# Windowed transformer on Trainium2: row-shift copies in eight pieces, two attention tiles without unused fronts, feed-forward rows normalised by ScalarE

## Chip, cores and metric

One core of one Trainium2 chip. The metric is the device time of one execution in microseconds (us). Three runs of the kernel before are shown, and one execution of it was profiled.

## What is computed

The program has four stages on x of shape (2, 2048, 128). The last one, with more than seven tenths of the time, is the only one that the change touches: a transformer of six layers over a window of 32 positions, with 16 heads of 64. Its reference, cut to what matters:

```python
def shift_tokens(t):
    a, s = jnp.split(t, 2, -1)
    s = jnp.pad(s, ((0, 0), (1, 0), (0, 0)))[:, :-1]
    return jnp.concatenate([a, s], -1)

def attn_layer(x, Wqkv, qs, ksc, Wo):
    q, k, v = jnp.split(x @ Wqkv, 3, -1)          # then 16 heads of 64
    q, k = l2norm(q) * qs, l2norm(k) * ksc
    q = q * cos * scale + rotate_half(q) * sin * scale
    k = k * cos / scale + rotate_half(k) * sin / scale
    return local_attention(q, k, v) @ Wo          # own window of 32 and the one before

def ffn_layer(x, g, bln, W1, b1, W2, b2):
    xn = (x - mean(x)) / jnp.sqrt(var(x) + 1e-05) * g + bln
    a, gate = jnp.split(xn @ W1 + b1, 2, -1)      # 341 units each
    return a * jax.nn.gelu(gate, approximate=False) @ W2 + b2

for i in range(DEPTH):                            # DEPTH = 6
    x = attn_layer(shift_tokens(x), ...) + x
    x = ffn_layer(shift_tokens(x), ...) + x
```

## The kernel before

All of it is in `windowed_transformer` (L1170), written in Bass with one program for each engine and semaphores between them; the order of each engine's work is written out by hand. A tile is 128 positions (J = 16 of them) of one batch row (B = 2): U = 32 tiles a layer, called units here, numbered u = 2 j + b. The residual lies in SBUF in two parts: its left 64 columns in `xs`, its right 64 in `xb`. The token shift of the right half is a copy by DMA: `xb` shifted down by one partition into columns 64 to 127 of `xs`, by `shift` (L1403, 127 partitions) and `shift_rows` (L1407, the row that crosses to the next tile), both on SyncE's queue. At the stage's start all 16 positions' tiles go in one pair; in a layer one pair follows each two units of attention, and one pair each of the eight groups of the feed-forward. SyncE also copies `early_values` (L1411): the values of the window before a tile, that the attention of half the windows reads.

A layer starts with a **prologue** (L1524 on GpSimd, L1672 to 1684 on TensorE). GpSimd copies a tile of `xs` to `x_tile`, TensorE transposes it and projects it with Wqkv in six chunks of 512 columns, three matmuls each for precision. ScalarE squares the q and k chunks, VectorE turns them (L1965: times the rotary tables) and sums the squares. GpSimd adds the two rotary terms (`rotate`, L1464), makes the inverse norm of k (`floor_k`, `newton_k`) and scales (`scale_k`, `scale_q`). Then comes the **loop over the 32 units**, in which each engine works two tiles ahead: while unit u is attended, the k and q of u+1 are transposed, and u+2 is transposed, projected, squared and turned. The part that serves later tiles is called a tile's front. Before, it runs in every unit, for tiles 32 and 33 too, whose results are not used. A unit ends with `residual` (L2005).

The **feed-forward** takes eight groups of G4 = 4 units. For each group VectorE makes statistics (`group_stats`), variance, an inverse root in ten Newton steps (`group_rstd`, L64 to 82, started from an integer), and normalises the rows (`group_normalise`, L2090). TensorE transposes them (L1726); ScalarE applies the layernorm's scale and bias and rounds (`split_group`, L1918, L1920) and VectorE makes the low part (L2095). `hidden_units` (L1742) has three chunks of hidden units, gate columns in bank S and value columns in bank PT, three matmuls each. ScalarE applies Gelu (L1937), VectorE multiplies (`gate`, L2101), `outputs` (L1769) multiplies by W2, and VectorE adds to the residual (`add_outputs`, L2146), two groups later. Meanwhile GpSimd prepares the next layer's attention (`prepare_attention`, L1313: weights split in two at L1329 and L1331, tables scaled at L1336).

What sets the order at the seams: the feed-forward's first statistics stand behind the last unit's residual on VectorE, and the first x tile of the next layer waits for the last piece of the shift:

```python
pool.wait_ge(shift_main, DMA * (l * SHIFTS + 1))      # with one increment at the start
pool.wait_ge(shift_row, DMA * (l * SHIFTS + 1))       # and SHIFTS = J + GROUPS a layer
nc.gpsimd.tensor_copy(xcur[:], xs[:, 0, 0, :])        # L1524
```

## Time and profile before

| | us |
|---|---|
| median of 3 runs | 5956.59 (5954.01 to 5966.02) |
| the profiled execution | 5959.97 |
| its span, first to last instruction | 5958.0 |
| mean granted TensorE clock (1 is full speed) | 0.909 |
| busy: TensorE matmul, VectorE, ScalarE, GpSimd | 5089.0, 4327.4, 3775.4, 2536.1 |
| windowed stage, its six layers' first transposes | 1626.7, 2344.9, 3059.6, 3775.0, 4490.0, 5205.9 |

The rows of the trace use these names: PE is TensorE, PEld its weight load, DVE VectorE, ACT ScalarE, POOL GpSimd, SP SyncE, and SPq SyncE's DMA queue. Buffers of this stage begin with d_. "out<-in" are an instruction's operands, x and a number its count, and a bracket at the end says how long the engine stood idle before it and what released it. Times are microseconds from the span's start, a mean of one is in ns. Layer 0 is the first of the six, and its unit 31 ends with the residual at about 2229.

### The profile page before, as it was taken

Reading aid. Unit: us, or ns where it says so; the run is one execution under the profiler, and the core shown is the slowest. Engines: PE = TensorE matmul, PEld = TensorE weight load, DVE = VectorE, ACT = ScalarE, POOL = GpSimd, SP = SyncE. Lnnn points to the kernel's source line nnn. Section 1 sums busy time; section 2 is a strip of 40 time slices with the busy share of each in tenths; the row PEclk is TensorE's granted clock in tenths of the full one; section 3 lists DMA queues with packets and bytes.
Section 4 is the critical chain, followed back from the end, with each engine's and each line's share of the span. In section 5 each row is a group of like instructions: output and inputs, shape, how many; then the busy total and the mean of one; then the engine's idle time right before and its main releaser. Section 6 shows DMA issues by size and latency. Waiting matters only on the chain. (4 is left out here: it accounts for less than half of the span.)

```text
span 5958.0 us, 148484 instructions
## 1 busy us (share of the span) xinstructions
PE 5089.0 (85%) x41656; PEld 4226.5 (71%) x41656; DVE 4327.4 (73%) x11808; ACT 3775.4 (63%) x12267; POOL 2536.1 (43%) x3943
## 2 busy tenths in 40 slices
PE   5987868997089996999869998799987999689994
PEld 3665767986078874888758886588866888578883
DVE  4454575776578886788868888688886888778887
ACT  1112433342089983899749996599956999389982
POOL 0000000000266662666626665466645666266661
PEclk7786887998599997999989998899988999899997
DMA  0000110000111111011101111111111111111111
GB/s 19 0 0 14 44 27 1 0 0 1 43 24 26 23 30 39 22 25 26 47 20 24 27 23 45 24 24 24 26 43 25 26 23 24 46 24 23 26 25 49
DMA packets 103769, 146.50 MB, mean 25 GB/s; under 512 B 65414, under 2 KB 72859, under 8 KB 103131
## 3 DMA queue, kind: packets, MB, share of 16 engines
q1 hardware_dynamic: 94155, 109.63, 8.1%
q0 software_dynamic: 9232, 33.12, 1.7%
q14 instruction: 307, 2.51, 0.1%
q8 instruction: 75, 1.23, 0.1%
HBM read 49.13 MB, written 2.10 MB: 9 GB/s over the span
## 5 line engine op out<-in xcount | busy, mean ns | idle before, releaser
L1841 ACT ACTIVATE d_probs<-d_S_ps,d_neg_max 128x96 f32<-128x96 f32 x3096 | 1008.4, 342 | 69.3 <-issue 57.7
L1470 POOL TENSOR_TENSOR d_qk<-d_qk,d_sin_terms 128x512 f32<-128x512 f32 x792 | 989.3, 1271 | 14.1 <-DVE d_sin_terms L1965 14.1
L1628 PEld LDWEIGHTS d_S_ps<-d_kT,d_q_blocks 128*128 128x128 f32 x6240 | 806.7, 193 | 2.5
L1628 PE MATMUL d_S_ps<-d_kT,d_q_blocks 128*128 128x96 f32 x6240 | 805.3, 272 | 0.0
L1965 DVE TENSOR_TENSOR d_qk<-d_A_ps,d_tables 128x512 f32<-128x512 f32 x816 | 560.2, 686 | 218.1 <-ACT d_squares L1797 146.9
L1841 ACT ACTIVATION_READ_ACCUMULATOR d_probs<-d_S_ps,d_neg_max 128x1 f32 x3096 | 644.8, 208 | 0.0
L1585 PE MATMUL d_A_ps<-d_wqkv_hi,d_xT_hi 128*128 128x512 f32 x1212 | 586.1, 484 | 17.3 <-DVE d_sin_terms L1965 12.3
L1797 ACT ACTIVATE d_squares<-d_A_ps 128x512 f32<-128x512 f32 x816 | 491.7, 603 | 133.9 <-PE d_A_ps L1587 133.6
L1965 DVE TENSOR_TENSOR d_sin_terms<-d_A_ps,d_tables 128x512 f32<-128x512 f32 x816 | 554.7, 680 | 0.0
L1592 PE MATMUL d_T_ps<-d_ident,d_qk 128*128 128x128 f32 x3168 | 501.3, 282 | 50.4 <-POOL d_qk L1507 45.2
L1849 ACT ACTIVATE d_probsT<-d_PT_ps 96x512 f32<-96x512 f32 (+1 forms) x768 | 460.3, 599 | 70.3 <-PE d_PT_ps L1638 69.8
L1955 DVE TENSOR_REDUCE d_sum_squares<-d_squares 128x16 f32<-128x1024 f32 x402 | 486.8, 1211 | 18.5 <-issue 17.9
L1587 PE MATMUL d_A_ps<-d_wqkv_lo,d_xT_hi 128*128 128x512 f32 x1212 | 487.4, 402 | 0.0
L1586 PE MATMUL d_A_ps<-d_wqkv_hi,d_xT_lo 128*128 128x512 f32 x1212 | 486.0, 401 | 0.0
L1638 PE MATMUL d_PT_ps<-d_ident,d_probs 128*96 128x128 f32 (+1 forms) x3072 | 464.6, 274 | 0.0
L1507 POOL TENSOR_TENSOR d_qk<-d_qk,d_inv_norm 128x1024 f32<-128x1024 f32 x198 | 376.8, 1903 | 182.6 <-DVE d_inv_norm L1987 182.2
L1592 PEld LDWEIGHTS d_T_ps<-d_ident,d_qk 128*128 128x128 f32 x3168 | 363.0, 144 | 121.6 <-issue 50.2
L2002 DVE TENSOR_TENSOR d_probs<-d_probs,d_PT_ps 128x384 f32<-128x384 f32 x768 | 425.3, 554 | 26.5
L1993 DVE TENSOR_REDUCE d_neg_max<-d_S_ps 128x4 f32<-128x384 f32 x780 | 427.4, 548 | 14.0 <-PE d_S_ps L1628 14.0
L1661 PE MATMUL d_PT_ps<-d_wo,d_attnT 128*128 128x128 f32 x3072 | 393.0, 281 | 0.0
L1661 PEld LDWEIGHTS d_PT_ps<-d_wo,d_attnT 128*128 128x128 f32 x3072 | 357.3, 191 | 40.9 <-issue 40.9
L1507 POOL TENSOR_TENSOR d_qk<-d_qk,d_k_inv_norm 128x1024 f32<-128x1024 f32 x198 | 377.0, 1904 | 15.1
(404 smaller groups left out, 11227.0 us busy)
## 6 DMA issues: line engine op xcount, KB each, us to landing
d_v_early<-d_v SPq DMA_DIRECT2D x198, 256.0 KB, 3.0
d_v_early<-d_v SPq DMA_DIRECT2D x198, 128.0 KB, 2.3
d_tables<-L_ffn_rotary POOLq DMA_DIRECT2D x7, 2048.0 KB, 9.7
d_qk<-L_ffn_Wqkv POOLq DMA_DIRECT2D x21, 512.0 KB, 4.1
d_xs<-d_xb SPq DMA_DIRECT2D x96, 63.5 KB
d_xs<-d_xb SPq DMA_DIRECT2D x48, 127.0 KB
ax_fp_blocks<-L_ffn_blocks_gu SPq DMA_DIRECT2D x16, 256.0 KB, 3.8
ax_fp_scales<-L_ffn_scales_gu SPq DMA_DIRECT2D x64, 64.0 KB, 3.3
```

Source lines behind the costliest of these rows:

```text
L1470: nc.gpsimd.tensor_tensor(c4[:, :, s, :], c4[:, :, s, :], s4[:, :, 1 - s, :], ALU.add).then_inc(rotated, 1)
L1507: nc.gpsimd.tensor_tensor(r3, r3, inverse.unsqueeze(2).broadcast_to([P, HEADS, HD]), ALU.mult).then_inc(scaled, 1)
L1585: nc.tensor.matmul(bank[:], xh[:], wh[:, sl], start=True, stop=False)
L1586: nc.tensor.matmul(bank[:], xl[:], wh[:, sl], start=False, stop=False)
L1587: nc.tensor.matmul(bank[:], xh[:], wl[:, sl], start=False, stop=True).then_inc(proj_ps, 1)
L1592: last = nc.tensor.transpose(T0[:, p * P:(p + 1) * P], raw[:, k, col:col + P], ident[:])
L1628: last = nc.tensor.matmul(S[g % 2][:, n * SEEN:(n + 1) * SEEN], qx[:, p, half, :], kT[b][jj][:, p, HALF * half:HALF * half + SEEN], start= ...
L1661: last = nc.tensor.matmul(Y[:, 0:D], oT[:, p, :], wo[:, p, :], start=(p == 0), stop=(p == 7))
L1797: nc.scalar.activation(sq[:, k, half * 512:half * 512 + 512], A[(c + 1) % 2][:], ACT.Square).then_inc(proj_squared, 1)
L1841: nc.scalar.activation(pr[:, g, n, seen_columns(g)], S[g % 2][:, n * SEEN:(n + 1) * SEEN], ACT.Exp, bias=nmax[:, g, n:n + 1], accum_out=de ...
L1955: nc.vector.tensor_reduce(ssq[:, k, :, 0], sq[:, k, :].rearrange("p (h d) -> p h d", d=HD), AX.X, ALU.add).then_inc(ssq_ready, 1)
L1965: nc.vector.tensor_tensor(terms[:, k, cols].rearrange("p (h d) -> p h d", d=HD), A[(c + 1) % 2][:].rearrange("p (h d) -> p h d", d=HD), ta ...
```

## The change

1. **Shift copies.** The first shift is eight pairs of two positions each, and a pair waits until the one before has landed. In the layers, each of the feed-forward's pieces waits for the piece before it. The semaphore counts are so placed that a unit's x tile waits for the piece that holds it, in the first layer one of the eight and in later layers the feed-forward's piece of its own group (`next_x`, in GpSimd's program). `early_values` of layer 0 stand behind the eight pairs on SyncE's queue.
2. **Last two units.** The loop body takes `lead`: 2 is the full front, 1 (unit 30) has no x tile, projection, squares or turns, 0 (unit 31) has no front. The loop is seven times four units, and four more are written out (`tiles_of_layer`).
3. **Feed-forward begun in unit 31.** Statistics, variance, inverse roots of groups 0 and 1, the normalising, transposing and splitting of group 0 stand between the attention steps of unit 31 (`last_tile`). VectorE waits for the last pieces of the attention's shift only before group 2.
4. **Normalised by ScalarE.** ScalarE computes xn as x times rstd plus a shift, minus mean times rstd, in four Identity activations at the head of its group, ahead of the Gelus. Rsqrt's start value also comes from ScalarE (`group_guess`). VectorE runs nine dependent Newton steps in a row, each with one operand in PSUM (bank A1), and one that makes the shift. `gate` of chunk 0 stands ahead of `add_outputs`.
5. **GpSimd.** In the prologue rotate and scale of k come before rotate of q, and rotate k before `floor_k`. The loads of W1 wait for the feed-forward before. `prepare_attention` starts after the last transposes of k and q, in unit 31, and loads Wo at its end.

The diff, cut to its core:

```diff
-        XS = U + 2
+        XS = U
+        def tiles_of_layer(engine, tile):
+            with engine.Fori(0, J // 2 - 1) as i:
+                for jj in range(2):
+                    for b in range(B):
+                        tile(i * 2 + jj, jj, b, pair=i)
+            tile(J - 2, 0, 0)
+            tile(J - 2, 0, 1)
+            tile(J - 1, 1, 0, lead=1)
+            tile(J - 1, 1, 1, lead=0)
...
-                shift(0, J, shift_main)
-                shift_rows(0, J)
+                for g in range(GROUPS):
+                    if g:
+                        sp.wait_ge(shift_main, DMA * g)
+                        sp.wait_ge(shift_row, DMA * g)
+                    shift(g * 2, 2, shift_main)
+                    shift_rows(g * 2, 2)
...
                         sp.wait_ge(resid_f, (l * GROUPS + g) * 2 + 6)
+                        sp.wait_ge(shift_main, DMA * (l * SHIFTS + (GROUPS + J) + g))
+                        sp.sem_inc(waits_met)
                         shift(g * 2, 2, shift_main)
                         sp.wait_ge(f_xn, (l * (GROUPS + 1) + g) * 4 + 8)
+                        sp.wait_ge(shift_row, DMA * (l * SHIFTS + (GROUPS + J) + g))
+                        sp.sem_inc(waits_met)
                         shift_rows(g * 2, 2)
...
                     pool.wait_ge(tab_ready, (l + 1) * 4)
+                    rotate(l, 0, 1)
                     floor_k(l, 0)
                     newton_k(l * XS, 0)
-                    rotate(l, 0, 1)
+                    scale_k(f0, l * XS, 0)
                     rotate(l, 0, 0)
-                    scale_k(f0, l * XS, 0)
                     scale_q(f0, 0)
...
+                    def next_x(l, u, j, b, group):
+                        if b == 0:
+                            pool.wait_ge(shift_main, DMA * (l * SHIFTS + (group + 1)))
+                            pool.sem_inc(waits_met)
+                            pool.wait_ge(shift_row, DMA * (l * SHIFTS + (group + 1)))
+                            pool.sem_inc(waits_met)
+                        pool.wait_ge(xT_ps, l * XS + u)
+                        pool.sem_inc(waits_met)
...
-                    pool.wait_ge(wo_ps, (l + 1) * U)
                     pool.wait_ge(proj_turned, (l + 1) * TURNS_IN_LAYER)
-                    prepare_attention(pool, l + 1, (l + 1) % DEPTH)
+                    pool.wait_ge(qk_T_ps, (l + 1) * (FRONTS * 4))
+                    pool.sem_inc(waits_met)
+                    prepare_attention(pool, l + 1, (l + 1) % DEPTH, last_use=(l + 1) * U)
...
+                    def group(g, gp):
                         q = l * GROUPS + g
+                        act.wait_ge(f_xT_ps, m0 + (g + 1))
+                        group_normalise(g + 1, s0 + (g + 1), 1 - gp)
                         for c, (o, sz) in enumerate(FF_CHUNKS):
...
-                        act.wait_ge(f_a_ps, q * 3 + 3)
-                        split_group(m0 + g + 1)
+                        split_group(m0 + (g + 1))
+                        group_guess(s0 + (g + 2))
...
+                    def group_rstd(ms, gp):
+                        v.wait_ge(f_guess, ms + 1)
+                        for i in range(3):
+                            var, step, root = (fve_ps, fst_ps, frt[:]) if i == 0 else (fve[:], frt2[:], frt_ps)
...
+                            nc.vector.tensor_tensor(step, var, root, ALU.mult).then_inc(f_newton, 1)
...
+                    def last_tile(j, jj, b):
...
+                        normalise(l, u, 0)
+                        find_max(l, u, 2)
...
+                        group_stats(0, s0)
+                        group_variance(s0, 0)
+                        normalise(l, u, 1)
+                        find_max(l, u, 3)
+                        group_rstd(s0, 0)
+                        normalise(l, u, 2)
+                        group_stats(1, s0 + 1)
+                        group_variance(s0 + 1, 1)
+                        normalise(l, u, 3)
+                        split_group_low(m0)
+                        group_rstd(s0 + 1, 1)
+                        residual(a, j, b)
...
+                    def group(g, gp, residual=True):
+                        q = l * GROUPS + g
+                        gate(q, gp, 0)
+                        if residual:
+                            for half in range(2):
+                                add_outputs(g - 2, gp, half)
+                        gate(q, gp, 1)
+                        gate(q, gp, 2)
+                        group_stats(g + 2, s0 + (g + 2))
+                        split_group_low(m0 + (g + 1))
+                        group_variance(s0 + (g + 2), gp)
+                        group_rstd(s0 + (g + 2), gp)
```

What stands in a row on an engine's queue, before and after (line numbers of the changed kernel where it is the changed kernel's). First SyncE at the start of the stage, before: the one pair, then the early values of unit 0 (v_early, 32 partitions and 64).

```order
L1403 DMA d_xs<-d_xb 127x32x64
L1407 DMA d_xs<-d_xb 1x32x64
L1420 UNCONDITIONAL_BRANCH
L1420 ISA
L1413 ISA
L1415 DMA d_v_early<-d_v 32x1024
L1416 DMA d_v_early<-d_v 64x1024
L1422 UNCONDITIONAL_BRANCH
```

After, the last three of the eight pairs, and then the early values:

```order
L1420 DMA d_xs<-d_xb 127x4x64
L1424 DMA d_xs<-d_xb 1x4x64
L1420 DMA d_xs<-d_xb 127x4x64
L1424 DMA d_xs<-d_xb 1x4x64
L1420 DMA d_xs<-d_xb 127x4x64
L1424 DMA d_xs<-d_xb 1x4x64
L1442 UNCONDITIONAL_BRANCH
L1442 ISA
L1431 ISA
L1433 DMA d_v_early<-d_v 32x1024
L1434 DMA d_v_early<-d_v 64x1024
L1461 UNCONDITIONAL_BRANCH
```

The early values stand behind every pair. Second, ScalarE's loop body of the feed-forward, one group, before (squares is Gelu's output, S_ps its input; qk and ff_xT_hi are the split of the next group):

```order
L1934 REGISTER_ALU
L1937 ACTIVATE d_squares<-d_S_ps,d_vectors 128x512
L1931 REGISTER_ALU
L1937 ACTIVATE d_squares<-d_S_ps,d_vectors 128x512
L1936 REGISTER_ALU
L1937 ACTIVATE d_squares<-d_S_ps,d_vectors 85x512
L1917 ISA
L1918 ACTIVATE d_qk<-d_T_ps,d_vectors 128x512
L1920 ACTIVATE d_ff_xT_hi<-d_qk 128x512
L1928 REGISTER_ALU
L1928 COMPARE_AND_BRANCH
```

and the same place after, up to the first Gelu:

```order
L1951 REGISTER_ALU
L1955 ISA
L1955 ACTIVATE d_qk<-d_xs,d_ff_shift,d_ff_rstd 128x128
L1955 ISA
L1955 ACTIVATE d_qk<-d_xs,d_ff_shift,d_ff_rstd 128x128
L1955 ISA
L1955 ACTIVATE d_qk<-d_xs,d_ff_shift,d_ff_rstd 128x128
L1955 ISA
L1955 ACTIVATE d_qk<-d_xs,d_ff_shift,d_ff_rstd 128x128
L2040 ISA
L2043 REGISTER_ALU
L2046 ACTIVATE d_squares<-d_S_ps,d_vectors 128x512
```

Four normalisings of rows of xs, with their operands of VectorE, came ahead of the three Gelus. Third, ScalarE in unit 31 after the change, from the second half of probs (the exponentials of the last set come first):

```order
L1908 ACTIVATE d_probsT<-d_PT_ps 128x512
L1896 REGISTER_ALU
L1900 ACTIVATE d_probs,d_den<-d_S_ps,d_neg_max 128x96 x4
L1974 ISA
L1951 REGISTER_ALU
L1955 ACTIVATE d_qk<-d_xs,d_ff_shift,d_ff_rstd 128x128 x4
L1908 ACTIVATE d_probsT<-d_PT_ps 96x512
L1911 REGISTER_ALU
L1913 ACTIVATE d_attnT<-d_O_ps 128x4x64
L1978 REGISTER_ALU
L1959 ISA
L1960 ACTIVATE d_qk<-d_T_ps,d_vectors 128x512
```

The normalising of group 0 and its split stand between the drains of the attention; before, they came behind unit 31's last.

## Rows read from the trace of the kernel before

**Rows 1.** Page, part 1: busy us of the engines, share of the span, instructions.

```profile
PE 5089.0 (85%) x41656; PEld 4226.5 (71%) x41656; DVE 4327.4 (73%) x11808; ACT 3775.4 (63%) x12267; POOL 2536.1 (43%) x3943
```

**Rows 2.** Stretches of layer 0: us, then PE, PEld, DVE, ACT, POOL, PEclk, DMA, GB/s.

```profile
1566.90:1626.70 59.80, 0.00 (x0) 0.00 (x0) 0.00 (x0) 1.28 (x1) 0.01 (x1) 0.50 0.08 18
1684.00:1947.00 263.00, 259.50 (x2504) 218.40 (x2503) 213.47 (x538) 240.76 (x854) 171.55 (x271) 1.00 0.11 25
2211.40:2229.00 17.60, 17.05 (x167) 14.23 (x165) 14.50 (x38) 16.07 (x57) 8.48 (x16) 1.00 0.10 23
2229.00:2241.30 12.30, 1.15 (x5) 0.78 (x5) 10.32 (x40) 2.41 (x3) 7.27 (x8) 0.57 0.84 271
2241.30:2316.40 75.10, 58.45 (x299) 45.77 (x299) 61.24 (x199) 24.74 (x37) 16.80 (x9) 0.84 0.08 22
2299.84:2316.39 16.55, 15.28 (x95) 12.24 (x94) 14.59 (x61) 6.93 (x10) 0.00 (x0) 1.00 0.07 16
2316.40:2344.90 28.50, 10.42 (x73) 8.88 (x71) 10.71 (x47) 4.75 (x6) 0.29 (x1) 0.73 0.08 19
```

**Rows 3.** Waits, whole windowed stage: total us, times, longest.

```profile
POOL d_x_tile L1524 <- DMA d_xs<-d_xb: 449.7, 6, 76.7
DVE d_ff_tmp L80 <- DMA d_xs<-d_xb: 30.5, 6, 6.4
```

**Rows 4.** Timeline at the stage's start: start us, us, engine, line.

```profile
1567.89 56.54 SPq L1407 DMA_DIRECT2D d_xs<-d_xb  x1
...
1671.10 0.69 PE L1652 MATMUL d_O_ps<-d_probsT,d_v_early 96*64 96x64 f32 x16
```

**Rows 5.** Timeline, prologue of layer 1, VectorE's last turn of k, then GpSimd.

```profile
2350.34 0.68 DVE L1965 TENSOR_TENSOR d_sin_terms<-d_A_ps,d_tables 128x512 f32<-128x512 f32 x1
...
2352.42 0.24 POOL L1476 TENSOR_SCALAR d_k_sums<-d_sum_squares 128x16 f32<-128x16 f32 x1 [4.55 <-DVE d_sum_squares L1955]
...
2356.93 4.88 POOL L1470 TENSOR_TENSOR d_qk<-d_qk,d_sin_terms 128x512 f32<-128x512 f32 x4
2361.77 1.90 POOL L1507 TENSOR_TENSOR d_qk<-d_qk,d_k_inv_norm 128x1024 f32<-128x1024 f32 x1
```

**Rows 6.** Lines of the attention loop, 1684 to 1947: busy, mean ns | idle.

```profile
L1841 ACT ACTIVATE d_probs<-d_S_ps,d_neg_max 128x96 f32<-128x96 f32 x239 | 77.9, 342 | 5.0 <-issue 4.3
...
L1797 ACT ACTIVATE d_squares<-d_A_ps 128x512 f32<-128x512 f32 x60 | 36.2, 603 | 7.5 <-PE d_A_ps L1587 7.5
```

**Rows 7.** Timeline, feed-forward's start in layer 0.

```profile
2234.42 3.22 DVE L2090 TENSOR_SCALAR d_qk<-d_xs,d_ff_mv,d_ff_rstd 128x128 f32<-128x128 f32 x4
...
2241.83 0.63 PE L1756 MATMUL d_S_ps<-d_ff_xT_hi,d_w_lo 128*128 128x512 f32 x1
```

**Rows 8.** Lines of the feed-forward, 2283 to 2316.

```profile
L1937 ACT ACTIVATE d_squares<-d_S_ps,d_vectors 128x512 f32<-128x512 f32 (+1 forms) x12 | 8.2, 686 | 13.7 <-PE d_S_ps L1757 12.2 <-DVE d_sin_terms L2101 1.6
L2101 DVE SCALAR_TENSOR_TENSOR d_sin_terms<-d_PT_ps,d_vectors,d_squares 128x512 f32<-128x512 f32 x8 | 5.9, 743 | 0.0
...
L1756 PE MATMUL d_PT_ps<-d_ff_xT_hi,d_w_lo 128*128 128x512 f32 (+1 forms) x12 | 4.7, 394 | 0.0
...
L2090 DVE TENSOR_SCALAR d_qk<-d_xs,d_ff_mv,d_ff_rstd 128x128 f32 x16 | 4.5, 342 | 0.4 <-DVE d_ff_rstd L82 0.3
...
L80 DVE SCALAR_TENSOR_TENSOR d_ff_rstd<-d_ff_rstd,d_ff_ve 128x4 f32<-128x4 f32 x8 | 1.3, 164 | 0.3
```

**Rows 9.** Timeline, from the last additions of layer 0 to layer 1.

```profile
2327.61 0.41 DVE L2146 TENSOR_TENSOR d_xb<-d_A_ps,d_xb 128x256 f32<-128x256 f32 x1
...
2336.22 6.08 SPq L1407 DMA_DIRECT2D d_xs<-d_xb  x1
...
2344.57 0.29 POOL L1524 COPY d_x_tile<-d_xs 128x128 f32<-128x128 f32 x1 [76.69 <-DMA d_xs<-d_xb]
```

**Rows 10.** Timeline, feed-forward of layer 0: GpSimd and VectorE side by side.

```profile
2258.61 6.97 POOL L1336 TENSOR_TENSOR d_tables<-d_tables,d_qk_scale 128x1024 f32<-128x1024 f32 x3 [0.18 <-POOL d_wqkv_lo L1331]
...
2258.68 2.31 DVE L80 SCALAR_TENSOR_TENSOR d_ff_rstd<-d_ff_rstd,d_ff_ve 128x4 f32<-128x4 f32 x1
```

More of the change, by code:

```diff
@@ L1938, in _ @@
                                                  bias=vecs[0:sz, 5 + c:6 + c]).then_inc(f_gelu, 1)
-                        act.wait_ge(f_a_ps, q * 3 + 3)
-                        split_group(m0 + g + 1)
+                        split_group(m0 + (g + 1))
+                        group_guess(s0 + (g + 2))
+                    with act.Fori(0, GROUPS // 2) as i2:
+                        for gp in range(2):
+                            group(i2 * 2 + gp, gp)
             @block.vector
@@ new lines, in tile @@
+                    def tile(j, jj, b, lead=2, pair=None):
+                        if not lead:
+                            last_tile(j, jj, b)
+                            return
+                        u = j * 2 + b
+                        a = l * U + u
+                        f1 = f0 + (u + 1)
+                        if lead:
+                            sum_squares(l, u + 1, 0)
+                            floor_sums(l, u + 1)
+                        normalise(l, u, 0)
+                        find_max(l, u, 2)
+                        if lead:
+                            newton_steps(f1, 1 - b)
+                        if lead == 2:
+                            split_x_low(l * XS + (u + 2))
+                        normalise(l, u, 1)
+                        find_max(l, u, 3)
+                        normalise(l, u, 2)
+                        if lead == 2:
+                            turn(l, u + 2, 0, j + 1)
+                            sum_squares(l, u + 2, 1)
+                        normalise(l, u, 3)
+                        if lead == 2:
+                            turn(l, u + 2, 1, j + 1)
+                        if lead:
+                            find_max(l, u + 1, 0)
+                        if lead == 2:
+                            turn(l, u + 2, 2, j + 1)
+                        if lead:
+                            find_max(l, u + 1, 1)
+                        if lead == 2:
+                            turn(l, u + 2, 3, j + 1)
+                        residual(a, j, b)
@@ L2097, in gate @@
+                    tiles_of_layer(v, tile)
                     def gate(q, gp, c):
```

406 lines of the change are left out of this document (217 added, 189 removed).

## Prediction

> **What bounds the kernel now.** I read the busy time of the engines first, then stretches of the first of the six layers, then the instructions at each seam. No engine is full: TensorE is busy 5089 of 5958 us, VectorE 4327, ScalarE 3775 [rows 1]. So the stages between differ, and the table of stretches says how [rows 2]. In the attention loop (1684 to 1947 us) TensorE is busy 259.5 of 263 us at a granted clock of 1.00: that loop is full, and only doing less in it pays. The seams are not. While the right half of the residual is shifted at the start, nothing runs for 59.8 us; the stretch from the last tile's residual to the first feed-forward matmul is 12.3 us with 1.15 us of TensorE; the one from the last group's first matmul to the next layer is 28.5 us with 10.4. In the feed-forward's steady part (two groups, 16.55 us) TensorE has 15.28 and VectorE 14.59: period 8.3 us, but the whole of it takes 75.1 where 7 periods would be 58. The waits over all layers confirm it is every layer: GpSimd waits for a shift before its first x tile 6 times, 449.7 us in total (it is idle before, so this is place, not price), and VectorE 6 times, 30.5 us, inside the feed-forward [rows 3].
>
> **Part 1, the first shift.** One row-shift transfer of 16 tiles takes from 1567.89 for 56.5 us [rows 4]: the DMA share is 0.08 and 18 GB/s [rows 2], one engine's worth, so cutting it gives no bandwidth. Each of eight pieces then costs 1/8 of it, 7.1 us, and a wait for landing; a late piece in the feed-forward stands 6.08 us in its row copy alone [rows 9], and with its issue ahead of it and the landing behind comes to about 9.4 us. The first x tile is therefore free at about 1576 instead of 1626: 50 us of head start. But SyncE's queue holds the copies of the early values behind all eight pieces: 7 x 9.4 + 7.4 = 73 us, so it is free at about 1641 and they land by 1645. Before, unit 0 first used them at 1671.1 [rows 4]. Everything ahead of that use can run early, then TensorE's in-order queue stands until 1645. Gain 1671 - 1645 = **26**.
>
> **Part 2, the prologue.** GpSimd now rotates k before its own Newton chain and scales k before rotating q. k is turned at 2351.0; before, GpSimd idled until the sums at 2352.4, ran its chain to 2356.9, rotated both (4.88) and scaled k by 2363.67 [rows 5]. Now: 2351.0 + 2.44 + 4.5 + 1.9 = 2359.9. q is then done only 1.3 us earlier, but TensorE has a projection between. Gain 3.8 in five layers (the first is bound by part 1): **19**.
>
> **Part 3, unit 30** has no x tile, projections, squares or turns for a tile 32 that no one reads. A unit takes 17.6 us with TensorE at 17.05 and ScalarE at 16.07 [rows 2]. ScalarE loses four squares of 0.603 [rows 6], a guess and a split, 3.0 us; TensorE loses more. ScalarE's remaining chain sets it: 14.8. Gain 2.8 x 6 = **17**.
>
> **Part 4, unit 31 and the start of the feed-forward.** Before, 17.6 + 12.3 = 29.9 us [rows 2]. The 12.3 is one chain on VectorE: statistics, Newton steps, a normalise of 3.22 us, then transpose and split [rows 7]. Now this chain stands inside a tile without any front. Its VectorE work is four maxima and normalisings (4.0), two groups' statistics and Newton (6.8), split and residual (1.3); with its hand-overs to ScalarE's exponentials (0.342 each and a read behind it, four to a set [rows 6]) I get a chain of 15.9. I add 1.3, since GpSimd's weight preparation now starts inside this tile: the normalise took 3.22 for four where 0.342 each is usual [rows 7, 8], while GpSimd subtracted. Gain 29.9 - 17.3 = 12.6, x 6 = **76**. Bounds: 9 (all of GpSimd's tensor_tensors in the way) to 14 (none).
>
> **Part 5, the feed-forward**, 75.1 us now. What goes: 6.4 us in the first layer, 5.1 on average, of VectorE standing before group 0 for tile 15's shift [rows 3] (it now waits before group 2), and the locked stretch: 2.31 us for an instruction of 4 elements a partition that else takes 0.164, under three GpSimd multiplications of 6.97 us [rows 8, 10]; some ten us a layer. What comes: ScalarE's queue has four normalisings ahead of the first Gelu (1.4 us, taken as long as VectorE's of the same tiles, 0.342 each [rows 8]), and these wait for VectorE's last step of the group before. VectorE was busy 7.3 us in a group [rows 2]; without its normalisings and with one more copy and a vector it is 6.2. Its ten dependent steps of 0.16 and more, ScalarE's guess ahead of them (0.3) and the hand-overs of three gates (0.743 [rows 8]), split and variance I put at 1.3 us of standing: 7.5 in all. Then normalise 1.4 and Gelu 0.686 stand in the way before the next gate: 9.6, of which 0.1 overlaps. Before, the Gelus only waited for TensorE (12.2 of 13.7 us [rows 8]). So the steady group becomes **9.5, slower than 8.3**. First two groups 7.1 + 9.8, five of 9.5, 3 for locks that remain: 67.4. Gain 7.7 x 6 = **46**. Bounds: -4 (all at 9.9, 6 of locks) to 17 (8.2 a group).
>
> **Part 6, into the next layer.** Before, the first x tile waited for the last piece: copied at 2344.57, when the piece whose rows were issued at 2336.22 had landed, though the additions were done at 2328.0 [rows 9]. Now it waits only for the first group's piece. TensorE's first transpose follows its last output matmuls (about 10.8 us after H7, the last group's first matmul), the additions and a split: 13.7 instead of 28.5. Gain 14.8 x 5 = **74**. Bounds: 11 to 16 each.
>
> **Part 7, costs.** Each feed-forward piece waits for the one before, which takes 9.4 us: a cadence of 9.5 keeps pace, except at the end, where two additions come close together; the last piece of layer 6 lands 4 us later against its addition. **-4.** GpSimd's new waits in the loop I put at nothing: its sequencer gets there while scale_k, 1.9 us, runs [rows 5]. Without that cover 0.5 us in every other unit, 96 x 0.5, at most 48.
>
> Sum: 26 + 19 + 17 + 76 + 46 + 74 - 4 = 254. The profiled execution took 5959.97 (span 5958.0): 5706. The median of the three runs is 5956.59, 3.4 lower: **5703**.
>
> **Rivals.**
> (a) The steady group stays at 8.2 (VectorE's tail hidden because TensorE's output matmuls fill it): 5 x 1.3 x 6 = 39 more, **5664**. For it: VectorE's own work hardly grows. Against: ScalarE's in-order queue. 0.18.
> (b) TensorE's clock falls in the feed-forward. Each group would have a wait of about 2 us. The table shows 1.00 in the steady groups, 0.57 across the seam and 0.84 over the whole [rows 2], and a 512-column matmul takes 0.63 at the low level against 0.394 [rows 7, 8]. At 1.2 GHz a group's 7.6 us of TensorE become 12.2, period 12.5: 3.0 x 7 x 6 = 126 more, **5829**. Against: a group with 80% busy. 0.10. The Trainium skill, "TensorE: Matmul & The Clock Gate", section "HAM oscillation", speaks against the change: bursts of matmuls with a wait between them can be thrown back to the low clock each time. No stretch of this trace with such short waits shows that.
> (c) The early values don't stall layer 0, or pieces land faster than 9.4: up to 24 more, **5679**. 0.10.
> (d) The change does not do what it says at the seams: with eight pieces at 9.4 us each and a group faster than that, x tiles and groups still wait for the transfers; parts 4 and 6 give half: **5778**. Against: only the wait for the own group is named. 0.07.
> (e) Slower than before: the attention loop, full at clock 1.00, loses it. At 1.2 GHz its 17 us of TensorE would take 1.6 times that, 10 us more a unit; it decides when 26 of the 192 units run so, and gives with 40 of them **6100**. Against: its body is the same instructions. 0.03.
>
> My forecast has 0.52. Range: 5703 + (7 x 6 in part 5, 3.6 x 6 in part 4, 19 of part 7) is 5785; the lower end takes (a), half of (c) and some of the upper bounds of parts 4 and 6 (12), **5640**. Outside it are (b), (e) and some of (d). A difference under 0.2%, 12 us, could not be told from no change here. Faster 0.96, within 0.01, slower 0.03.
>
> **What would show it.** The first windowed matmul near 1578, but the first attend of unit 0 near 1645. In a prologue, k transposed about 3.8 us earlier after layer start. Unit 30 at 14.8; first feed-forward matmul 17 us after unit 30's residual. In the steady group Gelu 0 waiting behind ScalarE's normalise, TensorE idle some 2 us, period 9.5, clock 1.00. The next layer's transpose 13.7 after H7. Wrong would be: a period of 12 at a clock of 0.5 (b), or 8.2 (a); x tiles of a layer still waiting for a DMA (d).

## The result, and the profile after

The changed kernel takes **5803.6 us** (median of 4 runs, 5800.2 to 5807.0) beside 5961.3 for the kernel before on the same chip (4 runs): a ratio of 0.9733, 95% interval 0.9712 to 0.9753. It is faster, as forecast, but by 158 us and not by 254: 5803.6 lies above the range that ended at 5785. The profiled execution took 5800.15, its span is 5798.4 against 5958.0, 159.6 less, and this difference can be split up stretch by stretch.

The page of the changed kernel, part 1, answers to [rows 1]:

```profile
span 5798.4 us, 146909 instructions
...
PE 5025.7 (87%) x41260; PEld 4183.0 (72%) x41260; DVE 4110.3 (71%) x11388; ACT 3810.7 (66%) x12357; POOL 2461.0 (42%) x3763
```

TensorE gave up 63 us of work, VectorE 217, and ScalarE took over 35. The stretches of layer 3 answer to [rows 2] (us, then PE, PEld, DVE, ACT, POOL, PEclk, DMA share, GB/s): unit 30, unit 31 to the first feed-forward matmul, the feed-forward to the last group's first matmul, in it the stretch from group 1 to group 2, two steady groups, and from the last group to the next layer:

```profile
4233.14:4249.75 16.61, 14.26 (x154) 12.12 (x152) 7.92 (x28) 13.82 (x52) 7.13 (x6) 1.00 0.13 30
4249.75:4267.07 17.32, 11.08 (x119) 9.50 (x119) 11.35 (x55) 14.03 (x47) 9.40 (x9) 0.90 0.60 190
4267.07:4342.59 75.52, 56.01 (x299) 43.65 (x299) 47.43 (x166) 34.58 (x65) 14.34 (x8) 0.91 0.08 22
4276.23:4291.53 15.30, 11.53 (x47) 8.82 (x48) 9.80 (x28) 5.18 (x10) 7.63 (x4) 0.71 0.12 36
4301.50:4321.50 20.00, 15.43 (x95) 12.21 (x94) 12.75 (x53) 10.37 (x20) 0.28 (x1) 1.00 0.06 14
4342.59:4361.32 18.73, 10.63 (x73) 8.82 (x72) 9.69 (x43) 6.77 (x12) 0.00 (x0) 0.97 0.07 16
```

Unit 30 takes 16.61 where a unit took 17.3. Unit 31 and the start take 17.3 where 29.9 stood. But the feed-forward takes 75.5, no less than before, two steady groups 20.0 at full clock with TensorE idle for 4.6 of them, and the way into the next layer 18.7. Over all layers, measured between the same instructions in both traces (a layer's first transpose, the residuals of units 0, 29 and 30, each group's first matmul):

| part | before, us | after, us | gain in all | forecast |
|---|---|---|---|---|
| 1: the span's start to unit 0's residual | 1683.7 | 1656.6 | 27 | 26 |
| 2: prologue, layers 1 to 5, mean | 56.3 | 53.1 | 16 | 19 |
| loop, residual of unit 0 to 29, mean | 510.1 | 508.5 | 10 | 0 |
| 3: unit 30 | 17.3 | 16.6 | 4 | 17 |
| 4: residual of unit 30 to the first feed-forward matmul, mean | 29.8 | 18.4 | 69 | 76 |
| 5: group 0 to group 7, mean | 73.4 | 74.1 | -4 | 46 |
| 6: group 7 to the next layer, 5 times, mean | 28.5 | 19.4 | 45 | 74 |
| 7: group 7 of the last layer to the end | 66.4 | 73.9 | -8 | -4 |
| sum | | | 159 | 254 |

Of the missing 95 us, 50 are in part 5 and 29 in part 6. Row 1 holds 4.0 us that the change did not make: the stage's first copy left at 1562.9 instead of 1566.9. What happens in a steady group (layer 2, timeline; start us, us, engine, line):

```profile
3624.44 0.16 DVE L2187 SCALAR_TENSOR_TENSOR d_ff_shift<-d_ff_mv,d_ff_rstd 128x4 f32<-128x4 f32 x1
3624.82 1.65 ACT L1955 ACTIVATE d_qk<-d_xs,d_ff_shift,d_ff_rstd 128x128 f32 x4 [2.30 <-DVE d_ff_shift L2187]
3626.37 1.24 ACT L2046 ACTIVATE d_squares<-d_S_ps,d_vectors 128x512 f32<-128x512 f32 x2
...
3627.09 0.47 PE L1813 MATMUL d_S_ps<-d_ff_xT_hi,d_w_hi 128*85 128x512 f32 x1 [2.29 <-ACT d_squares L2046]
3627.16 0.75 DVE L2257 SCALAR_TENSOR_TENSOR d_sin_terms<-d_PT_ps,d_vectors,d_squares 128x512 f32<-128x512 f32 x1 [2.55 <-ACT d_squares L2046]
```

VectorE ends its last step, the shift vector, at 3624.60. ScalarE has stood idle for 2.30 us until then, because the normalising is next in its queue; it takes 1.65 us for it. Only then comes the Gelu (L2046) of this group's chunk 0, whose input TensorE had finished 3.6 us before, at 3622.72, and TensorE, which needs that bank for its third chunk, and VectorE, which needs the Gelu for its first gate, stand idle 2.29 and 2.55 us. VectorE's next shift vector is done at 3634.58 and the next turn begins: a ring of VectorE (7.4 us), the normalising (1.65) and one Gelu (0.69), with 0.2 us from VectorE to ScalarE and 0.1 back.

### The profile page after: what moved, and what is told of

The parts are those of the page before. It is cut to its first block and busy times, and to the rows that moved or that the text cites. A ratio compares the mean times of both kernels' runs of the same rounds, so it can differ in the third digit from the quotient of the medians.

```text
span 5798.4 us, 146909 instructions
## 1 busy us (share of the span) xinstructions
PE 5025.7 (87%) x41260; PEld 4183.0 (72%) x41260; DVE 4110.3 (71%) x11388; ACT 3810.7 (66%) x12357; POOL 2461.0 (42%) x3763
## 5 line engine op out<-in xcount | busy, mean ns | idle before, releaser
L1503 POOL TENSOR_TENSOR d_qk<-d_qk,d_sin_terms 128x512 f32<-128x512 f32 x768 | 960.9, 1273 | 30.6 <-DVE d_sin_terms L2078 30.6
L2078 DVE TENSOR_TENSOR d_qk<-d_A_ps,d_tables 128x512 f32<-128x512 f32 x768 | 527.5, 687 | 230.2 <-ACT d_squares L1856 163.0
L1634 PE MATMUL d_A_ps<-d_wqkv_hi,d_xT_hi 128*128 128x512 f32 x1152 | 560.2, 486 | 14.9 <-DVE d_sin_terms L2078 10.2
L1856 ACT ACTIVATE d_squares<-d_A_ps 128x512 f32<-128x512 f32 x768 | 462.4, 602 | 131.2 <-PE d_A_ps L1636 131.0
L2078 DVE TENSOR_TENSOR d_sin_terms<-d_A_ps,d_tables 128x512 f32<-128x512 f32 x768 | 522.5, 680 | 0.0
L1641 PE MATMUL d_T_ps<-d_ident,d_qk 128*128 128x128 f32 x3072 | 485.0, 281 | 31.9 <-POOL d_qk L1540 27.8
L2068 DVE TENSOR_REDUCE d_sum_squares<-d_squares 128x16 f32<-128x1024 f32 x384 | 465.1, 1211 | 18.5 <-issue 17.0
L1636 PE MATMUL d_A_ps<-d_wqkv_lo,d_xT_hi 128*128 128x512 f32 x1152 | 466.1, 405 | 0.0
L1635 PE MATMUL d_A_ps<-d_wqkv_hi,d_xT_lo 128*128 128x512 f32 x1152 | 465.9, 404 | 0.0
L1687 PEld LDWEIGHTS d_PT_ps<-d_ident,d_probs 128*96 128x96 f32 (+1 forms) x3072 | 352.8, 137 | 60.1 <-DVE d_probs L2115 26.3
```

Of the source, the lines that this page charges most:

```text
L1503: nc.gpsimd.tensor_tensor(c4[:, :, s, :], c4[:, :, s, :], s4[:, :, 1 - s, :], ALU.add).then_inc(rotated, 1)
L1634: nc.tensor.matmul(bank[:], xh[:], wh[:, sl], start=True, stop=False)
L1635: nc.tensor.matmul(bank[:], xl[:], wh[:, sl], start=False, stop=False)
L1636: nc.tensor.matmul(bank[:], xh[:], wl[:, sl], start=False, stop=True).then_inc(proj_ps, 1)
L1641: last = nc.tensor.transpose(T0[:, p * P:(p + 1) * P], raw[:, k, col:col + P], ident[:])
L1687: last = nc.tensor.transpose(PT[0][0:rows, n * P:(n + 1) * P], pr[:, g, n, 0:rows], ident[:])
```

## Experiments

All edits are made to the changed kernel unless said otherwise; "the group" is the time between two groups' first matmuls in the steady part, 10.0 us there.

**1. The normalising behind Gelu 0.**

```diff
-                        act.wait_ge(f_xT_ps, m0 + (g + 1))
-                        group_normalise(g + 1, s0 + (g + 1), 1 - gp)
                         for c, (o, sz) in enumerate(FF_CHUNKS):
+                            if c == 1:
+                                act.wait_ge(f_xT_ps, m0 + (g + 1))
+                                group_normalise(g + 1, s0 + (g + 1), 1 - gp)
```

> Edit: ScalarE's four normalisings of the next group stand between Gelu 0 and Gelu 1 instead of ahead of Gelu 0; nothing else. The changed kernel has a steady group of 10.0 us and 5803.6 us in all. Theory A (order: Gelu 0, which needs only TensorE, stands behind the normalising, which waits for VectorE's last step of the group before): the ring VectorE 7.4 + normalise 1.65 + Gelu 0.7 breaks, the steady group falls to 8.0 to 8.3, the last group's stretch to the last addition from 14.3 to about 12, saving 1.8 x 5 + 2 to 3 in each layer, 65 to 75 us: about 5735. Rival B (work: VectorE's ten dependent steps with ScalarE's guess make it the bound wherever the normalising stands): the group stays above 9.5 and the time within 10 us of the changed kernel's.

5728.6 us (4 runs, ratio to before 0.9594, 0.9577 to 0.9611), 75 below the changed kernel (83 by the two ratios: the kernel before stood at 5974 beside these runs). The group is 8.4, the way from group 7 to the last addition 12.8 instead of 14.3 to 15.7, group 0 to group 7 61.3 to 63.4 instead of 71.9 to 75.7. The same order of work as above, now (layer 3, timeline):

```profile
4258.78 0.69 ACT L2047 ACTIVATE d_squares<-d_S_ps,d_vectors 128x512 f32<-128x512 f32 x1 [0.21 <-PE d_S_ps L1815]
...
4260.48 0.16 DVE L2188 SCALAR_TENSOR_TENSOR d_ff_shift<-d_ff_mv,d_ff_rstd 128x4 f32<-128x4 f32 x1
...
4260.86 1.65 ACT L1955 ACTIVATE d_qk<-d_xs,d_ff_shift,d_ff_rstd 128x128 f32 x4 [1.39 <-DVE d_ff_shift L2188]
...
4261.16 0.75 DVE L2258 SCALAR_TENSOR_TENSOR d_sin_terms<-d_PT_ps,d_vectors,d_squares 128x512 f32<-128x512 f32 x1 [0.52 <-PE d_PT_ps L1815]
```

Gelu 0 comes 0.21 us behind its matmul. The normalising still waits 1.39 us for the shift vector, but only Gelu 1 stands behind it. Theory A holds and B falls: the same instructions on VectorE, and 1.6 us a group less. I expected 8.0 to 8.3; Gelu 1 still waits for VectorE, see 8.

**2. One Newton round less.**

```diff
-        F_STEPS = 9
+        F_STEPS = 6
-                        for i in range(3):
+                        for i in range(2):
```

> Edit: the feed-forward's inverse root takes two Newton rounds instead of three, six dependent steps instead of nine; the order on ScalarE stays. The output changes in its last digits by it. Theory A: the steps lie in the ring, so the steady group falls by their whole length, 3 x 0.195 = 0.6, from 10.0 to 9.4, and the time by about 0.6 x 8 x 6 = 28 us. A rival by which the group's 10.0 us is set by TensorE and its clock (C): no change of the group, 5798 in the profiled span.

Span 5767.7, 31 less than 5798.4 (28 expected). Groups of 9.4, less by the whole length of the three steps; in each layer one or two later groups took 11.0, with a granted clock of 0.84 or 0.85. VectorE's steps lie in the ring, and so does whatever is put into it.

**3. VectorE normalises in the loop again.** ScalarE's loop loses the normalising, and VectorE gets it between the additions and gate 1:

```diff
+                        v.wait_ge(f_xT_ps, m0 + (g + 1))
+                        xg = rows_of(g + 1)
+                        for t in range(G4):
+                            nc.vector.tensor_scalar(xn[:, t, :], xg[:, t, :], fmv[:, 1 - gp, t, 0:1], frs[:, 1 - gp, t:t + 1],
+                                                    ALU.subtract, ALU.mult).then_inc(f_xn, 1)
                         gate(q, gp, 1)
```

> Edit: inside the feed-forward's loop VectorE normalises the next group's rows again, between the additions and gate 1, as before the change; ScalarE's loop has only Gelus, split and guess. All else is the changed kernel. Theory A (ScalarE's order makes the 10.0 us): VectorE gets 1.1 to 1.4 us more work, 7.4 + 1.2 = 8.6 to 8.9 a group, below 10.0, though VectorE does more: 6 to 8 us a layer less, a span near 5755. Rival B (VectorE's serial steps are the bound): the group grows to 11.

Span 5731.5, 67 less; groups of 8.4 and 8.9 in turn (7.9 and 8.6 in the kernel before). VectorE now does more (two groups):

```profile
4276.40:4293.79 17.39, 15.42 (x96) 12.17 (x94) 14.76 (x61) 7.53 (x12) 0.00 (x0) 1.00 0.06 14
```

14.76 us of VectorE in 17.39, where the changed kernel had 12.75 in 20.0. Giving the work to the less busy engine cost 1.3 us a group, because of where it stood in that engine's queue.

**4. The tables hardly scaled.**

```diff
-                t3 = tabs[:, a, 0:J * HD].rearrange("p (j d) -> p j d", d=HD)
+                t3 = tabs[:, a, 0:HD]
```

> Edit: GpSimd's four multiplications of the rotary tables by q_scale and k_scale are done for the first of 16 positions only (64 elements a partition instead of 1024), so these are left out for the other positions. In the changed kernel they take 9.75 us inside group 1 of each layer, where the stretch from group 1's first matmul to group 2's is 12.9 to 16.4 us. If they lock VectorE out there, that stretch falls to about 10.0 and the layer gains 5; 6 layers: 25 to 30 us off the time, about 5772 in the span. If the stretch is long for another reason (the wait before group 2 for the last attention piece), it stays at 15 and the time at 5798.

Span 5751.6, 47 less, but 6.6 of them lie ahead of the stage's first transpose; group 0 to group 7 alone gave 32 in the six layers, where 25 to 30 were expected. Group 1 to group 2 had taken between 12.9 and 16.4 us and took 10.0 or 10.1 in all layers (one group of 11.2 or 11.3 follows in each, with its clock at 0.85), and group 0 to group 1 took 7.2 in layers 1, 2, 3 and 5. What stood there in the changed kernel (layer 2, timeline):

```profile
3583.50 9.75 POOL L1350 TENSOR_TENSOR d_tables<-d_tables,d_qk_scale 128x1024 f32<-128x1024 f32 x4 [0.18 <-POOL d_wqkv_lo L1345]
3583.69 2.69 DVE L2192 TENSOR_TENSOR d_ff_xT_lo<-d_qk,d_ff_xT_hi 128x512 fp32r<-128x512 f32 x1 [0.21 <-ACT d_ff_xT_hi L1962]
...
3586.71 1.93 DVE L2170 TENSOR_SCALAR d_ff_ve<-d_ff_mv 128x4 f32<-128x4 f32 x1
...
3590.84 0.16 DVE L2184 SCALAR_TENSOR_TENSOR d_ff_rstd<-d_ff_step,d_A_ps 128x4 f32<-128x4 f32 x1
3591.03 2.24 DVE L2187 SCALAR_TENSOR_TENSOR d_ff_shift<-d_ff_mv,d_ff_rstd 128x4 f32<-128x4 f32 x1
```

Under GpSimd's 9.75 us of multiplications, three VectorE instructions take 2.69, 1.93 and 2.24 us. The Newton steps between them, of the same size, take 0.16 or 0.17: each has an operand in PSUM. The granted clock was down there as well: 0.69 to 0.77 between group 1 and group 2 in the six layers, and 0.83 with the tables hardly scaled. What the block of VectorE costs by itself and what the clock costs on top of it, no run separates.

**5. TensorE's wait behind its branch.** The wait for the last additions moves from the end of the loop body to its head. The wait for the last Newton steps is left out; in the changed kernel it had been met at least 1.5 us before the last addition ended, in all five seams.

```diff
-                    pe.wait_ge(resid_f, (l + 1) * (GROUPS * 2) + 4)
-                    pe.wait_ge(f_newton, (l + 1) * ((GROUPS + 2) * F_STEPS))
...
+                    pe.wait_ge(resid_f, l * (GROUPS * 2) + 4)
                     pe.wait_ge(w_hi, (l + 1) * 3)
```

> Edit: TensorE's wait for the feed-forward's last additions stands at the head of the next layer instead of at the end of the loop body, so its branch back to the loop's head is taken before and not after the wait. The changed kernel's TensorE starts the next layer 4.2 to 4.4 us after the last addition ends, released by nothing that the profile shows. Theory: that is the branch back, with its instructions to be fetched, which used to lie under a wait of 16.9 us for the shift. Then the gap falls from 4.3 to about 1 to 2 us, 5 x 2.5 = 12 us off the time, span about 5786. If instead GpSimd's x tile or the loads are late, the gap stays at 4.3 and the span at 5798.

The changed kernel at the seam from layer 2 to 3:

```profile
3666.97 0.41 DVE L2265 TENSOR_TENSOR d_xb<-d_A_ps,d_xb 128x256 f32<-128x256 f32 x1
...
3671.56 0.47 PE L1721 MATMUL d_A_ps<-d_ident,d_x_tile 128*128 128x128 f32 x1 [5.60 <-issue]
```

The last addition ends at 3667.38 and TensorE starts at 3671.56, released by nothing. With the wait behind the branch, from layer 3 to 4:

```profile
4360.66 0.41 DVE L2265 TENSOR_TENSOR d_xb<-d_A_ps,d_xb 128x256 f32<-128x256 f32 x1
...
4362.24 0.32 PE L1722 MATMUL d_A_ps<-d_ident,d_x_tile 128*128 128x128 f32 x1 [2.59 <-issue]
```

from 4361.07 to 4362.24. In the five seams the gap is 0.6 to 1.2 us instead of 4.2 to 4.4, about 18 us in all, where 12 were expected. So some 3.6 of the 4.3 us belong to what stood behind the wait and now stands ahead of it, the branch back; GpSimd's x tile and the loads, which the edit left as they were, do not make them. Whether it is the branch itself or the fetching of instructions behind it is not shown. The span is 5792.9, only 5.5 less, but its first transpose came at 1586.6 instead of 1573.0: the part of the program ahead of this stage differs by up to 20 us between executions (1566.4 to 1586.8 in these runs), so single spans are not compared closer than that, and stretches are.

**6. Layer 0's early values behind two pairs.** SyncE copies those of unit 0 behind the second pair.

```diff
                     shift_rows(g * 2, 2)
+                    if g == 1:
+                        sp.wait_ge(v_copied, 2)
...
+                        sp.dma_start(early[0][WINDOW:SEEN, :], vals[0][0:HALF, 0, :]).then_inc(early_dma[0], DMA)
```

> Edit: SyncE copies the early values of layer 0's unit 0 behind the second of the eight pairs of shift copies instead of behind the eighth. In the changed kernel unit 0 of layer 0 ends 83.6 us after the layer's first transpose, in layers 1 to 5 52.9. Theory: the 30.7 us are SyncE's queue of eight pieces ahead of these copies, so layer 0 falls to 53 to 55 and the span by 28 to 30 us from 5798 (the start of the stage itself moves by some us between executions). Rival: in layer 0 the x tiles of the first units wait for their own pieces (one each 9.4 us, two positions each, four units), then at least 15 of the 30 stay.

In the changed kernel the eight pairs leave SyncE's queue at 1637.6 and the copies follow (timeline):

```profile
1562.94 0.92 SPq L1420 DMA_DIRECT2D d_xs<-d_xb  x1
1563.91 6.52 SPq L1424 DMA_DIRECT2D d_xs<-d_xb  x1
...
1630.28 0.75 SPq L1420 DMA_DIRECT2D d_xs<-d_xb  x1
1631.09 6.52 SPq L1424 DMA_DIRECT2D d_xs<-d_xb  x1
1638.09 0.61 SPq L1433 DMA_DIRECT2D d_v_early<-d_v  x1
```

With the edit the span is 5796.6, 1.8 less where 28 to 30 were expected; its first transpose came 13.8 us later than in the changed kernel. Layer 0's prologue fell from 83.6 to 53.6 us, all of the 30; but its loop grew from 508.7 to 526.1. The next unit's copies still stood behind the eighth pair, and TensorE waited there:

```profile
1660.35 1.12 PE L1713 MATMUL d_O_ps<-d_probsT,d_v_early 96*64 96x64 f32 x16 [15.23 <-DMA d_v_early<-d_v]
```

One wait took the place of the other, net 12.6 us. I had named neither this nor the right rival. In the second version of 8 the copies of units 0, 1 and 2 stand behind the second, fourth and sixth pair: prologue 52.6, loop 507.7.

**7. Unit 30.** First its queues reordered, then its q hardly scaled by GpSimd.

```diff
+                        if lead == 1:
+                            transpose_q(f1, 0)
...
+                                nc.gpsimd.tensor_tensor(raw[:, 0, 0:HD], raw[:, 0, 0:HD], rn[:, 1 - b, 0:1].broadcast_to([P, HD]),
+                                                        ALU.mult).then_inc(q_scaled, 1)
```

> Edit: in unit 30 alone TensorE transposes and attends probs 2 ahead of the q transposes, and probs 3 ahead of the next unit's scores; ScalarE takes the last exponentials, probs 2 and the attention's drain ahead of draining q. Unit 30 takes 16.6 us in the changed kernel where 14.8 was forecast from ScalarE's work. Theory: what holds it is the chain through GpSimd (q of unit 31 is scaled 6.9 us after the unit's start, as in every unit) and the in-order queues behind it, so taking unit 30's own work out from behind it gives about 1.5 us, unit 30 at 15.0 to 15.5, the span 5 to 9 us less. Rival: the unit is held by its own softmax chain, and stays at 16.6; or the work only moves, and unit 31 grows by what unit 30 loses.

> Edit: in unit 30 alone GpSimd scales one of 16 heads of q for unit 31 (64 columns instead of 1024), so 15 heads of these tiles' q stay unscaled; the rest is the changed kernel. The step takes 1.90 us there and ends 6.9 us after the unit's start; TensorE then transposes q, and ScalarE drains it ahead of the unit's last exponentials. Theory: this chain, not ScalarE's amount of work, holds unit 30 at 16.6 us; then the unit falls by about 1 to 1.7, to 15 to 15.6, and the residual of unit 31 comes no later. Rival: the unit's own softmax chain holds it; then 16.6 stays, or unit 31 grows by the same amount.

Both missed: the spans are 5805.7 and 5807.7, with their first transposes 9.5 and 11.4 us later than the changed kernel's, so nothing is left of a gain. Unit 30 took 15.9 us in the first, 16.2 in the second, with unit 31 at 16.6 to 18.8 and 15.9 to 18.1 (16.2 to 18.3 in the changed kernel). The stretch of unit 30 in layer 3 with its queues reordered:

```profile
4243.68:4259.62 15.94, 14.39 (x154) 12.11 (x152) 8.00 (x28) 13.55 (x52) 7.12 (x6) 1.00 0.14 31
```

and with q hardly scaled:

```profile
4246.23:4262.40 16.17, 14.29 (x154) 12.09 (x152) 7.91 (x28) 13.81 (x52) 5.51 (x6) 1.00 0.13 30
```

In the changed kernel ScalarE is busy 13.8 of 16.6 us and TensorE 14.3: neither is full. 1.6 us off the GpSimd step gave 0.4, and the order 0.7. My theory of the GpSimd chain explains a quarter of the 1.8 us between 14.8 and 16.6; the rest stays open, and no run separates it. Of the reordering's 0.7, 0.4 to 0.5 was lost again in unit 31 (its shortest 16.6 instead of 16.2, its longest 18.8 instead of 18.3), and it is left out of the later versions below.

**8. A better version.** Four edits together first: 1, 5, 6 and the reordering of 7.

> Edits together: the normalising between Gelu 0 and Gelu 1, TensorE's wait behind its branch, the early values behind the second pair, unit 30 reordered. If each stall lies on the path by itself, the gains add to that of the normalising alone (5728.6 us, 5712 in the profiled span): 29 for the early values, 17 for the branch (3.4 in 5 layers), 0 to 9 for unit 30: about 5680, 5660 to 5690.

5690.1 us (4 runs, ratio 0.9549, 0.9532 to 0.9566), the upper end of what was expected: layer 0's loop kept its 526. Then the normalising behind Gelu 1 (`if c == 2`), the waits of 5, three early copies spread, unit 30 as it was. In the layers, too, SyncE's copies of early values now stand behind a piece of the shift where they stood ahead of it, one pair of units earlier:

> Edits: the normalising stands between Gelu 1 and Gelu 2; TensorE's wait behind its branch; SyncE's early values of units 0, 1 and 2 of layer 0 behind the second, fourth and sixth pair of shift copies (the run with unit 0's alone won 30 us in the prologue and gave 17.6 back in unit 1, whose copies still stood behind all pairs); unit 30 as in the changed kernel (its reordering won 0.7 and lost 0.5 or more in unit 31). Expected against the run with four edits (5690.1 us, group 8.4): layer 0's loop back at 508 to 510 instead of 526.2, 17 us; Gelu 1 no longer waits for VectorE's last step, so the group falls to 7.9 to 8.2, 6 x 7 x 0.3 = 13 us; about 5660. If unit 1's loss had another cause than the queue, the loop stays at 526 and the time at 5677.

**5658.9 us** (5 runs, ratio 0.9482, 0.9469 to 0.9495). As expected, the group is 7.8 to 8.0; the gap at the seam is 0.6 to 1.1. On top of it two Newton rounds:

> Edits: those of the run with the normalising behind Gelu 1, and two Newton rounds instead of three in the feed-forward's inverse root. VectorE's loop (7.4 us of a group) should then be 6.8, and TensorE's 7.6 the bound. If VectorE's ring is still what sets the group, it falls by another 0.3 to 0.6 us, 6 x 8 x 0.4 = 20 us; if TensorE sets it already, nothing.

5648.1 us (4 runs, ratio 0.9460, 0.9446 to 0.9475), 11 less where 20 were expected. The group is 7.7, what TensorE's own work takes (15.43 busy in two groups, in the table of stretches). In place of that, means and variances in PSUM:

```diff
-        fmv = m.sb("ff_mv", [P, 2, G4, 2])
+        fmv = A[1][:, 4 * G4:8 * G4].rearrange("p (g t s) -> p g t s", g=2, t=G4)
```

> Edits: those of the run with the normalising behind Gelu 1, and the feed-forward's means and variances lie in PSUM bank A1 instead of SBUF, so that VectorE's variance and shift steps each read an operand from PSUM. In the changed kernel the variance step took 1.93 us and the shift step 2.24 instead of 0.16 under GpSimd's table multiplications, while the Newton steps beside them, each with an operand in PSUM, took 0.16. Theory: two SBUF sources make a VectorE step wait for the end of GpSimd's instruction. Then these two steps fall to about 0.2 and the stretch from group 1 to group 2 from 12.2 to 9.5 or so, 6 x 2.5 = 15 us off. Rival: it is GpSimd's instruction as such that blocks VectorE at fixed intervals; then another step is hit, and the stretch stays.

5645.1 us (4 runs, ratio 0.9459, 0.9441 to 0.9476), 14 less in the median where 15 were expected, but the intervals of the two ratios overlap, and one of the four runs took 5659.9. The stretches are clearer: group 0 to group 7 fell from 59.5 to 58.0 us in the mean, 9 us in six layers. VectorE's lines in layer 3's feed-forward, eight groups each (busy, mean ns), with the normalising behind Gelu 1:

```profile
L2204 DVE TENSOR_TENSOR d_ff_xT_lo<-d_qk,d_ff_xT_hi 128x512 fp32r<-128x512 f32 x8 | 5.8, 721 | 0.4
L2199 DVE SCALAR_TENSOR_TENSOR d_ff_shift<-d_ff_mv,d_ff_rstd 128x4 f32<-128x4 f32 x8 | 3.4, 425 | 0.3
L2182 DVE TENSOR_SCALAR d_ff_ve<-d_ff_mv 128x4 f32<-128x4 f32 x8 | 3.1, 388 | 0.3
```

and with the means in PSUM as well:

```profile
L2204 DVE TENSOR_TENSOR d_ff_xT_lo<-d_qk,d_ff_xT_hi 128x512 fp32r<-128x512 f32 x8 | 6.5, 818 | 0.4
L2182 DVE TENSOR_SCALAR d_ff_ve<-d_A_ps 128x4 f32<-128x4 f32 x8 | 1.3, 162 | 0.3
L2199 DVE SCALAR_TENSOR_TENSOR d_ff_shift<-d_A_ps,d_ff_rstd 128x4 f32<-128x4 f32 x8 | 1.3, 161 | 0.3
```

The variance step's mean fell from 388 to 162 ns and the shift step's from 425 to 161. Group 1 to group 2 had taken between 11.8 and 13.0 us (9.7 in layer 0) and took 9.2 to 9.9; with group 0 to group 1, which grew in three layers, the two fell from 20.1 to 18.4 in the mean. In what is left from group 1 to group 2 TensorE stands idle for 0.7 us at most, at a granted clock of 0.71 to 0.83: beside a steady group of 7.8 to 8.0 at 1.00 it is now the clock that makes it long. The subtraction that makes the low part, both sources in SBUF, is still hit (818 ns against 0.69 us undisturbed): one block remains of three. The rival, another step hit instead, holds for that share.

## Why the prediction was wrong, point by point

**Part 1, the first shift: right in its mechanism.** SyncE was free 75 us after its first copy (said 74), and TensorE first used the early values at 1641.9 (said 1645). That the gain is 27 against 26 is partly luck: the stage began 4.0 us earlier in this execution, and counted from its first copy the gain is 23.

**Part 2, the prologue: right,** 3.2 us a layer against 3.8.

**Part 3, unit 30: mis-sized,** 0.7 instead of 2.8 a layer. The step "ScalarE's remaining chain sets it: 14.8" counted work; ScalarE is busy 13.8 and the unit takes 16.6, so it stands idle for 2.8. The unit before also took 17.3, not the 17.6 that it started from.

**Part 4, unit 31: right in its mechanism,** 18.4 against 17.3. In layers 2 and 3 it was 17.1 and 17.3, at a granted clock of 0.90. In the other four it was 18.4 to 19.2, at 0.81 or 0.82; in two of these, layers 0 and 5, the split's subtraction also took 2.7 us under GpSimd. The run does not separate the two.

**Part 5, the feed-forward: this step failed.** Its mechanism was right, and it stood in the text: slower groups, by VectorE, the normalising and one Gelu in a ring (runs 1 to 3 show it). Of the 50 us that are missing here, 10 were never there: the 75.1 us that it subtracts from are layer 0's, and the mean of the six layers was 73.4. The other 40 are 6.7 a layer, 74.1 against 67.4, in three sizes. The group is 10.0 and not 9.5, 2.4 us in five groups: the normalising takes 1.65 us on ScalarE, where I took VectorE's time for it (1.4), and the two hand-overs beside it, 0.3 together, stood nowhere; VectorE's own 7.4 was met (said 7.5). "First two groups 7.1 + 9.8, 3 for locks that remain" is 19.9; measured 22.0 to 24.5, 23.5 in the mean, as GpSimd's table multiplications still fell into it (runs 4 and 8; in run 4, without most of them, 17.2 to 18.7) and the clock was down. And of the later groups one took 11.3 us in each of layers 2, 3 and 5, and two took 11.6 in layer 4, at a granted clock of 0.85; see rival (b).

**Part 6, into the next layer: the step "the additions and a split: 13.7" failed.** It had two things missing. The last group is slowed by the same ring, and for nothing: ScalarE normalises a ninth group, which no one uses, ahead of its Gelus, so the last addition ended 14.3 to 15.7 us after group 7's first matmul and not 11.6; in run 1, with it behind Gelu 0, 12.8. (The last groups of 15.3 to 15.7 are those of layers 0, 1 and 4, at a granted clock of 0.86; those of 14.3 were at 1.00.) And TensorE takes its branch back to the layer's head only after that addition, 4.2 to 4.4 us that the wait for the shift used to cover (run 5). I had read the wait of 17 us as the whole price of the seam, without asking what else lay under it. Of the 5.7 us a layer between 19.4 and 13.7, the last addition makes 3.4 and the branch, beside the 2.1 that 13.7 left behind the addition, 2.2.

**Part 7: mis-sized,** -8 instead of -4; 2.7 of the difference is the last group again. GpSimd's new waits cost nothing: the loop is 1.6 us a layer shorter, not longer, and I have no run that says why.

**The rivals.** (a) needed the ring not to bite; it did. (b), TensorE at 1.2 GHz throughout the feed-forward, did not come: the two steady groups in the table have a clock of 1.00, with 2.3 us of waiting in each. But a part of it did. Layer 2's group 6 in the changed kernel had 0.85 and took 11.3 us, behind one of 9.98 with the same work (stretches):

```profile
3631.76:3641.74 9.98, 7.69 (x49) 6.07 (x48) 6.36 (x27) 5.18 (x10) 0.00 (x0) 1.00 0.06 13
3641.74:3653.05 11.31, 9.03 (x49) 7.13 (x48) 6.44 (x27) 5.18 (x10) 0.00 (x0) 0.85 0.06 14
```

It had a wait of 2.3 us like the others. Over all traces, such falls go with the waits. Counted are the five stretches from group 2 to group 7 in each of six layers, 30 a run:

| trace | TensorE idle in such a group, us | of 30, with a clock of 0.84 or 0.85 |
|---|---|---|
| changed kernel, runs 4, 5, 6, both of 7 | 2.3 in most | 5, 6, 7, 9, 8 and 7 |
| run 2 | 1.7 in most | 7 |
| kernel before, runs 1 and 3, all four of 8 | 0 to 1.2 | none |

So the ring had a second price: about 1.3 us in each of five groups and three last groups, some 10 us in all (the third size of part 5, and the spread of the last groups in part 6). Which of the groups with the same wait falls, no run explains. The Trainium skill's section on "HAM oscillation" ("TensorE: Matmul & The Clock Gate") warns that a loop with a wait in each round can start every round at the low clock; its example waits 3 to 5 us a round. Here the trace agrees in the direction alone: the wait was in every group and the fall in one of six, and the price was 10 us and not the 126 us of the rival.

(c) became true in neither part, (d) not either: GpSimd still waits for a piece before the first x tile of layers 1 to 5, but copies it some 53 us before TensorE takes it (by 3618.9 for 3671.6 in layer 3), and the pieces in the feed-forward keep up with a group of 10.0. (e) did not happen, the clock in the loop is 1.00.

## What to carry to other kernels

When work moves to a less busy engine, look at what stands behind it in that engine's queue and at what it waits for: four normalisings of 0.41 us ahead of a Gelu closed a ring and cost more than they took off. When a long wait is removed, list all that lay under it (a branch back, a last group's unused work, another queue's copies), because the next of these becomes the new wait at once. And look whether an engine's busy time or its longest chain sets a stretch before giving a stretch the length of either.

## What the runs showed that I had not expected

- TensorE's way back to the head of a loop of this size took 4.2 to 4.4 us from a released wait to its first matmul, released by nothing in the profile; 0.6 to 1.2 us with the branch taken ahead of the wait.
- VectorE instructions of 4 elements a partition took 1.9 to 2.3 us with both sources, or the only one, in SBUF under a GpSimd tensor_tensor, and 0.16 us beside them with one source in PSUM. Moving one small operand to PSUM took the block away (388 to 162 ns, 425 to 161 ns in the mean of eight).
- Four Identity activations of 128x128 with scale and bias from vectors took 1.65 us on ScalarE (0.48 each, overlapping), against 4 x 0.342 for the same on VectorE.
- With TensorE idle for 1.7 or 2.3 us in most groups, the granted clock fell to 0.84 or 0.85 in 5 to 9 of 30 groups a run; with 1.2 us or less it fell in none, in seven traces each.
